# Attention stage on one Trainium2 core: maxima by single 128-row products, one turning per head, another last slot

## The reference, cut to what matters

```python
c_q = h_t @ W_DQ + b_DQ
c_kv = h_t @ W_DKV + b_DKV
q_c = (c_q @ W_UQ + b_UQ)      # per head 128 columns
k_c = (c_kv @ W_UK + b_UK)
v_c = (c_kv @ W_UV + b_UV)
q_r = (c_q @ W_QR + b_QR)      # per head 32 columns
k_r = (h_t @ W_KR + b_KR)      # 32 columns, shared by the heads
q = jnp.concatenate([q_c, q_r], axis=-1)
k = jnp.concatenate([k_c, k_r], axis=-1)
scores = jnp.einsum('bhsd,bhtd->bhst', q, k) * scale
attn = jax.nn.softmax(scores, axis=-1)
o = jnp.einsum('bhst,bhtd->bhsd', attn, v_c)
```

## Time and profile before

| what | us |
|---|---|
| median of 3 runs | 1053.29 |
| lowest and highest | 1051.64, 1056.0 |
| the profiled execution: its own time | 1043.46 |
| its span | 1041.7 |
| PE busy | 914.9 (88%) |
| DVE busy | 728.8 (70%) |
| ACT busy | 601.7 (58%) |
| POOL busy | 674.3 (65%) |

### The profile page before, as it was taken

How to read it: one execution, slowest core, us unless ns; L and a number is a source line. 1 busy time by engine, 2 the same in 40 slices (tenths; PEclk the granted TensorE clock), 3 DMA queues, 4 the chain that set the end, 5 groups by cost and what they waited for, 6 DMA issues and landing times. The chain is left out here.

```text
span 1041.7 us, 21977 instructions
## 1 busy us (share of the span) xinstructions
PE 914.9 (88%) x8662; PEld 551.4 (53%) x8662; DVE 728.8 (70%) x1344; ACT 601.7 (58%) x1004; POOL 674.3 (65%) x446
## 2 busy tenths in 40 slices
PE   4896899999999999999999987766089999999995
PEld 3442254454454454544544546655057776777664
DVE  5587788888888888888888845664146675557643
ACT  1231477777777777777777763445264466445650
POOL 4103988988988989889889893368514344533452
PEclk9898599999999999999999998996589999999998
DMA  9700000000000000000000004227824344524110
GB/s 267 287 1 1 1 2 3 1 2 2 2 1 2 2 2 2 2 2 2 2 2 2 2 2 162 81 105 239 276 95 163 116 144 149 178 88 164 49 49 19
DMA packets 47712, 69.46 MB, mean 67 GB/s; under 512 B 6928, under 2 KB 39893, under 8 KB 47610
## 3 DMA queue, kind: packets, MB, share of 16 engines
q1 hardware_dynamic: 37658, 50.95, 14.7%
q0 software_dynamic: 7680, 16.87, 4.9%
q10 hardware_dynamic: 2272, 0.24, 0.2%
HBM read 44.66 MB, written 29.66 MB: 71 GB/s over the span
## 5 line engine op out<-in xcount | busy, mean ns | idle before, releaser
L739 POOL TENSOR_TENSOR prob_lo<-prob 128x1024 f16<-128x1024 f32 x208 | 431.7, 2104 | 53.0 <-ACT prob L694 53.0
L768 DVE TENSOR_REDUCE part_max<-x_ps 128x1 f32<-128x512 f32 x512 | 330.0, 681 | 76.5 <-PE x_ps L625 74.0
L694 ACT ACTIVATE prob<-st_ps 128x512 f32<-128x512 f32 x512 | 305.3, 598 | 127.9 <-PE st_ps L615 120.8
L614 PE MATMUL st_ps<-QA,KA 128*128 128x512 f16 x512 | 199.0, 389 | 0.3 <-ACT prob L694 0.2
L615 PE MATMUL st_ps<-QB,KB 65*128 65x512 f16 x512 | 197.7, 386 | 0.0
L668 PE MATMUL acc_ps<-VV,prob 128*128 128x65 f16 x2048 | 159.2, 194 | 21.6 <-DVE both L793 17.6
L668 PEld LDWEIGHTS acc_ps<-VV,prob 128*128 128x128 bf16 x2048 | 141.8, 98 | 62.8 <-DVE both L793 32.9
L668 PE MATMUL acc_ps<-VV,prob_lo 128*128 128x65 f16 x2048 | 158.4, 194 | 0.0
L668 PEld LDWEIGHTS acc_ps<-VV,prob_lo 128*128 128x128 f16 x2048 | 134.5, 98 | 26.9 <-issue 0.3
L1250 POOL DMA_INDIRECT out<-yo,xb x48 | 47.9, 998 | 153.1 <-DVE yo L1357 150.4
L1280 ACT ACTIVATE act_f<-g_ps,cols 128x768 f32<-128x768 f32 x64 | 57.7, 901 | 104.3 <-PE g_ps L1403 104.3
(11 more groups left out here) (177 smaller groups left out, 1460.0 us busy)
## 6 DMA issues: line engine op xcount, KB each, us to landing
w1f<-in_L_ffn_w SPq DMA_DIRECT2D x8, 1024.0 KB, 4.8
w2f<-in_L_ffn_w SPq DMA_DIRECT2D x8, 1024.0 KB, 5.7
xbuf<-zeros SPq DMA_DIRECT2D x7, 910.0 KB, 13.7
xb<-xbuf SPq DMA_DIRECT2D x8, 780.0 KB, 5.5
x<-in_L_attn_h_t SPq DMA_DIRECT2D x4, 1024.0 KB, 10.5
out<-x SPq DMA_DIRECT2D x4, 1024.0 KB, 5.7
tbuf<-x SPq DMA_DIRECT2D x4, 1024.0 KB, 8.3
tbuf<-gb_row SPq DMA_DIRECT2D x4, 1024.0 KB, 5.1
```

Of the source, the lines that this page charges most:

```text
L614: mm(st_ps[i % 2][:], KA[:, at], QA[:, n % QRING, half], start=True, stop=False)
L694: nc.scalar.activation(prob[:, k, f * HALF:(f + 1) * HALF], st_ps[i % 2][:], ACT.Exp).then_inc(exp_done, 1)
L739: nc.gpsimd.tensor_tensor(prob_lo[:, k, :], prob[:, k, :], prob_top[:, k, :], ALU.subtract).then_inc(sub_pool, 1)
L768: nc.vector.tensor_reduce(part_max[:, item // 2, item % 2:item % 2 + 1], x_ps[i % 3][:], AX.X, ALU.max).then_inc(smax_done, 1)
```

## The change

Four edits, most of them in the attention block.

- The maxima are single products over all 128 rows of QA and KA (L631 of the changed kernel), so with the key's remainder. They stand one behind each half of the scores, and each waits for its own bank. KC, its copies on ACT and the ACT wait values that counted them are gone. The maxima of head p + 2 now fill slots 0 to 7 of head p (`FIRST_MAX = 0`), so that the whole-row maximum falls into slot 7.
- One turning a head: `mz` is 128 x 8 instead of 128 x 8 x 65, one product with the identity gives 8 x 128, in slot 1, between the first maximum and the second half of the scores. ACT copies it to `mrow` (8 x 128), and a DMA on SP's queue writes it as one row of 1024 to QB. The scores wait for that DMA.
- In slot 7 the values stand behind the first half of the scores, ahead of the slot's maxima. ACT copies `raw` and DVE adds `both` in that slot, no longer in slot 0 of the next head.
- The fill of `mz` with zeros on POOL is gone.

The core of the diff:

```diff
-        mz = sb(inner, "mz", [P, ST, LR + 1], fp16)
+        mz = sb(inner, "mz", [P, ST], fp16)
+        mrow = sb(inner, "mrow", [ST, 2, P], fp16)
...
-                    nc.scalar.activation(KC[LR:P, b, :], k_ps[LR:P, HALF:S], ACT.Identity, bias=bk[LR:P, :]).then_inc(hi_done, 1)
...
-        FIRST_MAX = 1
-        ROW_SLOTS = (2, 3)
+        FIRST_MAX = 0
+        ROW_SLOT = 1
...
+            @block.sync
+            def _(sp):
+                for n in range(HEADS):
+                    sp.wait_ge(mrow_done, n + 1)
+                    sp.dma_start(QB[LR:LR + 1, n % QRING, :].rearrange("a (t q) -> a t q", q=P),
+                                 mrow[:, n % 2, :]).then_inc(mrow_in[n % 2], 16)
...
-                        te.wait_ge(mrow_done, 2 * n + f + 1)
+                        te.wait_ge(mrow_in[n % 2], 16 * (n // 2 + 1))
...
-                    if i >= 2:
-                        te.wait_ge(smax_done, i - 1)
-                    te.wait_ge(qa_done, 2 * n + q // 4 + 1)
-                    at = slice(q * P, (q + 1) * P)
-                    mm(x_ps[i % 3][:], QA[0:LR, n % QRING, at], KA[0:LR, b * S:b * S + HALF], start=True, stop=True)
-                    mm(x_ps[(i + 1) % 3][:], QA[LR:P, n % QRING, at], KC[LR:P, b, :], start=True, stop=True).then_inc(smax_ready, 1)
+                    if i >= 3:
+                        te.wait_ge(smax_done, i - 2)
+                    te.wait_ge(qa_done, 2 * n + item // 8 + 1)
+                    at = slice(item // 2 * P, (item // 2 + 1) * P)
+                    part = slice(b * S + item % 2 * HALF, b * S + (item % 2 + 1) * HALF)
+                    mm(x_ps[i % 3][:], QA[:, n % QRING, at], KA[:, part], start=True, stop=True).then_inc(smax_ready, 1)
...
+                def max_rows(n):
+                    side_after_query(n + 1, 1)
+                    side_after_rows(n - 1)
                     te.wait_ge(max_done, n + 1)
-                    for q in range(4):
-                        last = mm(side_ps[0:LR + 1, q * P:(q + 1) * P], mz[:, 4 * f + q, :], ident16[:], start=True, stop=True)
-                    last.then_inc(mrow_ready, 1)
+                    mm(side_ps[0:ST, 0:P], mz[:], ident16[:], start=True, stop=True).then_inc(mrow_ready, 1)
...
                     for f in HALVES:
+                        if f == 1 and k == ROW_SLOT and is_head(p + 1):
+                            max_rows(p + 1)
                         if is_head(ns):
                             scores(ns, ks, f)
-                        if f == 0 and k in ROW_SLOTS and is_head(p + 1):
-                            max_rows(p + 1, ROW_SLOTS.index(k))
-                        if f == 0 and is_head(nm):
-                            maxima(nm, items[0] // 2)
+                        if f == 0 and k == ST - 1 and is_head(p):
+                            values(p, k)
+                        if is_head(nm):
+                            maxima(nm, items[f])
                     if k in QUERY_SLOTS and is_head(p + 3):
                         query(p + 3, QUERY_SLOTS.index(k))
-                    if is_head(p):
+                    if k < ST - 1 and is_head(p):
                         values(p, k)
...
-                    if k == 0 and is_head(p - 1):
-                        add_halves(p - 1)
+                    if k == ST - 1 and is_head(p):
+                        add_halves(p)
```

More of the change, by code:

```diff
@@ L292, in _ @@
                     nc.gpsimd.memset(dst, value).then_inc(const_p, 1)
-                pool.wait_ge(const_p, 15)
+                pool.wait_ge(const_p, 14)
                 pool.wait_ge(const_v, 2)
@@ L551, in adaln_block @@
         mrow_done = sem("mrow_done")
+        mrow_in = [sem(f"mrow_in{n}") for n in range(2)]
         raw_done = sem("raw_done")
@@ L615, in scores, with maxima @@
                     mm(st_ps[i % 2][:], KB[:, at], QB[:, n % QRING, half], start=False, stop=True).then_inc(scores_ready, 1)
-                def maxima(n, q):
-                    b = n // H
-                    i = n * 16 + 2 * q
-                    if i >= 2:
-                        te.wait_ge(smax_done, i - 1)
-                    te.wait_ge(qa_done, 2 * n + q // 4 + 1)
-                    at = slice(q * P, (q + 1) * P)
-                    mm(x_ps[i % 3][:], QA[0:LR, n % QRING, at], KA[0:LR, b * S:b * S + HALF], start=True, stop=True)
-                    mm(x_ps[(i + 1) % 3][:], QA[LR:P, n % QRING, at], KC[LR:P, b, :], start=True, stop=True).then_inc(smax_ready, 1)
+                def maxima(n, item):
+                    b, i = n // H, n * 16 + item
+                    if i >= 3:
[4 more added lines that the diff above has]
+                    mm(x_ps[i % 3][:], QA[:, n % QRING, at], KA[:, part], start=True, stop=True).then_inc(smax_ready, 1)
                 def side_after_query(n, f):
@@ L630, in side_after_query, with side_after_rows @@
                         te.wait_ge(ql_done, 2 * n + f + 1)
-                def side_after_rows(n, f):
+                def side_after_rows(n):
                     if n >= 0:
-                        te.wait_ge(mrow_done, 2 * n + f + 1)
+                        te.wait_ge(mrow_done, n + 1)
                 def query(n, f):
@@ L639, in query @@
                     if f == 0:
-                        side_after_rows(n - 2, 1)
+                        side_after_rows(n - 2)
                     else:
@@ L698, in query, with max_rows @@
                     nc.scalar.activation(QA[:, n % QRING, f * HALF:(f + 1) * HALF], side_ps[:], ACT.Copy).then_inc(qa_done, 1)
[L700 to L703, removed]
+                def max_rows(n):
+                    ac.wait_ge(mrow_ready, n + 1)
+                    if n >= 2:
+                        ac.wait_ge(mrow_in[n % 2], 16 * (n // 2))
+                    nc.scalar.activation(mrow[:, n % 2, :], side_ps[0:ST, 0:P], ACT.Copy).then_inc(mrow_done, 1)
                 def out_of_psum(n):
@@ L718, in _ @@
                             exponential(n, kk, f)
-                        if f == 0 and k in ROW_SLOTS and is_head(p + 1):
-                            max_rows(p + 1, ROW_SLOTS.index(k))
+                        if f == 0 and k == ROW_SLOT and is_head(p + 1):
+                            max_rows(p + 1)
+                        if f == 0 and k == ST - 1 and is_head(p):
+                            out_of_psum(p)
                     if k in QUERY_SLOTS and is_head(p + 3):
                         query(p + 3, QUERY_SLOTS.index(k))
-                out_of_psum(HEADS - 1)
             @block.gpsimd
@@ L764, in maxima @@
                     i = n * 16 + item
-                    v.wait_ge(smax_ready, i // 2 + 1)
+                    v.wait_ge(smax_ready, i + 1)
                     if item < 2 and n:
@@ L773, in whole_rows @@
                     if n:
-                        v.wait_ge(mrow_ready, 2 * n)
-                    nc.vector.tensor_reduce(mz[:, :, LR], part_max[:], AX.X, ALU.max).then_inc(max_done, 1)
+                        v.wait_ge(mrow_ready, n)
+                    nc.vector.tensor_reduce(mz[:], part_max[:], AX.X, ALU.max).then_inc(max_done, 1)
                 def query_low(n, f):
```

15 lines of the change are left out of this document (3 added, 12 removed).

## The result

| | before | changed kernel |
|---|---|---|
| median, us | 1053.91 (4 runs) | 1067.06 (4 runs) |
| lowest to highest | 1051.64 to 1056.0 | 1064.56 to 1067.29 |
| the profiled execution (its span) | 1043.46 (1041.7) | 1067.29 (1065.5) |

The ratio is 1.012, with a 95% interval from 1.0093 to 1.0146. The change makes the kernel slower, by some 13 us of the medians; the forecast for the changed kernel was 1073.9 us, and it took 1067.06. The two profiled executions lie 23.8 us apart, nearly twice as much as the medians. That leaves two questions.

A forecast was written before the change was run, and what follows sets the result against it. PE was taken to bound attention: a head 14.85 + 0.80 + 0.91 = 16.55 us against 15.89, +19.1 over 29 periods, +20.6 with the start; 1064.1 profiled, 1073.9 with 0.9% added. Range 1046 to 1082.

The forecast's parts named there:

- G: Small effects: dropped KC copies and mz fill, nothing; start of the attention stage, +1.5 us, between -1 and +3.
- A: Attention slots' maxima: two single 128-row products instead of a 64-row pair cost +0.01 us a slot, 0.1 a head.
- rival 4: Maxima on PE cost a whole product more a slot, +0.21 us over 240 slots, +50 in all: 1124; chance 0.01.
- B: One turning product for eight small ones a head: -0.375 us a head, the remaining 128-column product costing 0.055.
- C: Last slot's values, raw and both come earlier, so the 2.54 us slot 0 becomes a plain one: -0.755 a head.
- D: PE's turning in slot 1 waits for DVE's query_low, queued behind two maxima: 0.80 us a head, bounds 0.6 and 1.0.
- E: In slot 2 POOL's subtraction starts 0.16 us before DVE's and holds it up; PE waits 0.91 us a head.
- Rival 1: DVE's subtraction still gets in before POOL's, so PE's 0.91 us wait is absent: head 15.64, execution 1047.6; chance 0.14.
- F: The row's 2 KB DMA on SP's queue, needed by slot 4, taken as hidden: 4.1 us are there.
- rival 3: The row's transfer lands after 4.1 us; at 6.8 a head gains 1.8 us more: 1125; chance 0.05.
- the last of the sum: To the profiled execution's forecast of 1064.1 us, 0.9% added, its distance under the median of the runs: 1073.9.

The follow-up runs named there:

- the two repeats: The kernel before and the changed kernel, each run once more with no edit: 1058.83 us and 1066.87 us.
- the repeat: The changed kernel once more with no edit and more rounds: 1066.87 us (7 runs), ratio 1.0132 to the kernel before.
- the version that beats both: Changed kernel with DVE's query remainder ahead of slot 0's maxima and its subtractions at the start of slots 2 and 4: 1022.73 us, ratio 0.9646.

## Why the prediction was right, and where it was off

The sign, the two waits and their places came out; the median lies inside the range, 7 us under the forecast. The closeness of the total is in part luck, since errors of opposite sign cancelled (G and the last point).

- **A, the maxima.** Right for the slot: it takes 1.78 with single products, as with the pair. This speaks against rival 4 and against the speed of up to two times that the Trainium skill gives for 64-row tiling (TensorEngine Tiling (Array Packing), "Theoretical Speedup"). The 0.1 a head that was put down did not come. The working was incomplete otherwise: it weighed only PE's time, and in the kernel before the single products alone cost 0.94 a head, most of it by the race in slot 4. In the changed kernel that race goes well in slot 4 (DVE's subtraction takes 1.25 there).
- **B, one turning.** The term of the product was mis-sized: 0.055 was put down, the cost of one of its like in a row (0.056 when repeated), and a single one makes its slot 0.26 longer. So B saves some 0.2 a head less than forecast. Why the steps around a single small product are longer is not shown.
- **C, the last slot.** Right: slots 7 and 0 take 3.80 together (403.50 to 407.31), as a slot with a query and a plain one do, and the old order brings the wait back. A to C add up to 14.87 by their terms, where 14.85 was written, and 14.99 was measured without the waits; B's 0.2 and A's 0.1 account for it to about 0.02.
- **D, the turning waits for DVE.** 0.80 was forecast. The turning starts 0.81 later than 0.22 behind its forerunner, but 0.09 of this is its own longer step: slot 1 takes 2.76 against 2.04 without the wait, so the wait is 0.72, and taking it away gave 0.74. The walk had PE reach the turning that much too early.
- **E, DVE and POOL.** 0.91 was forecast, 0.93 found, and 0.94 gained when it was taken away. POOL was to come first by 0.16, and did by 0.15. Rival 1 falls, and the run with the subtraction 0.6 us earlier shows how near it was.
- **F, the transfer.** Right; rival 3 falls, with 1.82 us against the 4.1 that are there.
- **G, the start.** The missing KC copies changed nothing, as forecast: the first maximum comes at 97.47, and came at 97.53. For the start of the stage +1.5 was taken, between -1 and +3, and this was wrong in sign and outside its bounds. From the first maximum to the second `o_n` the time fell from 64.3 to 62.3, with the granted clock in that stretch at 0.84 instead of 0.76; in the two repeats it fell as much, from 62.7 (0.78) to 60.8 (0.86). Why the granted clock is higher there in the changed kernel was not tried. From the first maximum to the last `o_n` the stage grew from 531.3 us (97.53 to 628.86) to 551.1 (97.47 to 648.54), +19.7, of which the twenty-eight periods from the second `o_n` on give +21.8. So the stage's +20.6 is met to 1 us by two errors of opposite sign: a head cost 0.13 more than forecast (B's product is the main part of it), and the start some 3.6 less (-2.1 instead of +1.5). That is luck.
- **The step that was off most** is the last of the sum, where 0.9% was added because the profiled execution lay that much under the median. That distance is no property of the program: it was an execution of the kernel before with a short block behind attention. The profiled one of the changed kernel, forecast at 1064.1 and measured at 1067.29, is the longest of its four. The 3 us above the 1064.1 are the block behind attention, 129.4 against 125.5 us, less the 1 us of G. In three of the seven executions of the repeat the same kernel took 1079 us, on the other side of the 1073.9; the profiled one of these had 144.5 us in that block.

## What to carry to other kernels

When operations of two engines can shut each other out, what counts is not only each engine's own queue but which of the two operations starts first. Read from the trace which one that is and by how much. If it is 0.1 or 0.2 us, treat every edit that shifts an arrival, on any engine, as one that can flip it. Place the operation where the other engine surely is idle. When a step is moved to be early, list what it is put ahead of and which wait hangs on that; here the gain of a new slot order was given back (15.74 against 15.65) until one 0.67 us operation was moved too. And take the effect of an edit from the period of the loop that it changes, before looking at a median that holds an unrelated block with a scatter of 20 us.

## What the hardware showed that I had not expected

- The same block of the same program took 125 us at a granted clock of 0.80 and 139 at 0.68, in two executions of one kernel. In the version that beats both it took 139 as well (600 to 739, clock 0.68), and in one execution of the changed kernel 144.6, at 0.63.
- DVE needs 1.68 us instead of 1.21 for a subtraction that starts 0.01 behind POOL's 0.62 us scaling of 128x256: the short operation shuts it out too, and DVE ends 1.07 after it.
- One small product of 128 columns between large ones costs 0.26 us, and 0.056 behind its like.
- Two 64-row products that start together (404.07) take as much of PE's time, to 0.02 us, as two 128-row products one behind the other: the step ahead of the pair is 0.31 (from 403.76) and the one behind it 0.32 (to 404.39), where it is 0.22 between single products, and the plain slot is 1.78 us with either.
- 2 KB from SBUF to SBUF by an idle queue were usable 1.82 us after the issue began, which itself takes 0.64; the 128 KB loads that the prediction had to go by took 3.0 at least.
